# The value products of a step, moved behind the next step's first score

## What is computed

```python
q = (x @ q_w.T + q_b).reshape(B, S, H, Dh).transpose(0, 2, 1, 3)
k = (x @ k_w.T + k_b).reshape(B, S, H, Dh).transpose(0, 2, 1, 3)
v = (x @ v_w.T + v_b).reshape(B, S, H, Dh).transpose(0, 2, 1, 3)
q = apply_rope(q)
k = apply_rope(k)
attn = jnp.einsum('bhqd,bhkd->bhqk', q, k) * scaling
probs = jax.nn.softmax(attn, axis=-1)
out = jnp.einsum('bhqk,bhkd->bhqd', probs, v)
out = out.transpose(0, 2, 1, 3).reshape(B, S, D)
return out @ out_w.T + out_b
```

## Time and profile before

| | us |
|---|---|
| median of three runs | 868.22 |
| lowest, highest | 866.63, 878.57 |
| the profiled execution's own time | 867.31 |
| its span, first to last instruction | 865.6 |
| PE busy | 829.0 |
| DVE, ACT, POOL busy | 649.7, 525.2, 463.4 |
| mean granted clock of TensorE | 0.99 |

### The profile page before, as it was taken

How to read it: one execution, slowest core, us unless ns; L and a number is a source line. 1 busy time by engine, 2 the same in 40 slices (tenths; PEclk the granted TensorE clock), 3 DMA queues, 4 the chain that set the end, 5 groups by cost and what they waited for, 6 DMA issues and landing times.

```text
span 865.6 us, 14796 instructions
## 1 busy us (share of the span) xinstructions
PE 829.0 (96%) x4544; PEld 626.3 (72%) x4544; DVE 649.7 (75%) x1352; ACT 525.2 (61%) x1106; POOL 463.4 (54%) x397
## 2 busy tenths in 40 slices
PE   8899999999989999989998999999999989999997
PEld 6678788778878888766887888654434447888886
DVE  6898788999998888998386866757788644676553
ACT  4778788778868888763635442335566665454442
POOL 3565555666655556642666766522310526656774
PEclk9999999999999999999999999978999999999999
DMA  5233222322422323212765458311441133334451
GB/s 157 92 98 99 86 97 97 110 95 83 149 74 87 98 96 109 80 50 75 214 217 155 141 166 289 105 57 53 143 148 51 56 98 93 122 124 140 152 161 65
DMA packets 57442, 99.20 MB, mean 115 GB/s; under 512 B 8288, under 2 KB 19040, under 8 KB 57376
## 3 DMA queue, kind: packets, MB, share of 16 engines
q1 hardware_dynamic: 57376, 98.39, 35.5%
HBM read 71.88 MB, written 9.57 MB: 94 GB/s over the span
## 4 chain that ended last, share of the span: by engine, by line
PE 63%; POOL 10%; issue 10%; DVE 9%; ACT 4%; DMA 3%; SPq 0%; POOLq 0%; DVEq 0%; ACTq 0%
PE ps L986 10%; PE ps L972 9%; PE ps L963 9%; PE ps L321 5%; PE ps L387 5%; PE ps L335 4%; POOL q_sin L526 3%; PE ps L1654 3%; PE ps L375 3%; PE ps L348 3%; PE ps L1535 2%; PE ps L362 2%; POOL wqk_lo L520 2%; PE ps L1624 2%; DVE nm L1846 2%
## 5 line engine op out<-in xcount | busy, mean ns | idle before, releaser
L1110 POOL TENSOR_TENSOR ew_lo<-ew_raw,ew_hi 128x768 fp32r<-128x768 f32 x68 | 128.2, 1886 | 56.2 <-ACT ew_hi L1076 48.2
L1062 ACT ACTIVATE hid_hi<-guw 128x512 fp32r<-128x512 f32 x68 | 43.0, 632 | 156.6 <-POOL guw L1126 106.6
L1165 DVE TENSOR_TENSOR hid_lo<-guw,hid_hi 128x512 fp32r<-128x512 f32 x68 | 80.9, 1189 | 72.4 <-ACT hid_hi L1062 72.3
L1126 POOL TENSOR_TENSOR guw<-gu,cwb 128x512 f32<-128x512 f32 x61 | 80.5, 1320 | 91.3 <-issue 73.3
L526 POOL TENSOR_TENSOR q_sin<-q_sw,sin 128x512 f32<-128x512 f32 x62 | 80.7, 1312 | 52.5 <-DMA q_sw<-q_in 51.4
L1846 DVE TENSOR_REDUCE nm<-ps 128x1 f32<-128x512 f32 x128 | 81.6, 684 | 24.3 <-PE ps L1558 23.1
L1741 ACT ACTIVATE e<-ps 128x512 f32<-128x512 f32 x128 | 68.8, 602 | 40.3 <-PE ps L1654 40.1
L986 PE MATMUL ps<-ew_hi,hid_hi 128*128 128x256 f32 x272 | 78.3, 288 | 2.4 <-DVE hid_lo L1165 1.8
L512 DVE SCALAR_TENSOR_TENSOR w<-ex,rden,sgn 128x512 f32<-128x512 f32 (+3 forms) x128 | 79.0, 678 | 0.0
L438 ACT ACTIVATE ex<-sabs,nmax 128x512 f32<-128x512 f32 (+3 forms) x128 | 61.5, 551 | 27.9 <-DVE nmax L486 27.9
L986 PE MATMUL ps<-ew_hi,hid_lo 128*128 128x256 f32 x272 | 76.8, 282 | 0.0
(11 more groups left out here) (190 smaller groups left out, 2404.9 us busy)
## 6 DMA issues: line engine op xcount, KB each, us to landing
ew_raw<-in_ew SPq DMA_DIRECT2D x68, 384.0 KB, 3.3
q_sw<-q_in SPq DMA_DIRECT2D x128, 128.0 KB, 2.0
cwb<-cw_dram SPq DMA_DIRECT2D x61, 256.0 KB, 3.6
wqk_raw<-in_wqk SPq DMA_DIRECT2D x32, 256.0 KB, 2.7
wv_raw<-in_wv SPq DMA_DIRECT2D x32, 128.0 KB, 2.6
wo_raw<-in_wo SPq DMA_DIRECT2D x32, 128.0 KB, 2.2
qs<-stk_q SPq DMA_DIRECT2D x16, 256.0 KB, 3.6
ks<-stk_k SPq DMA_DIRECT2D x16, 256.0 KB, 4.2
```

What stands on the lines that cost most here:

```text
L1110: pool.tensor_tensor(ff[f].ew[1][:, i % EW_SLOTS, :], ew_raw[:, i % RAW_SLOTS, :], fp(ff[f].ew[0][:, i % EW_SLOTS, :]), ALU.subtract).then ...
L1126: pool.tensor_tensor(ff[f].guw[:, i % 2, :], ff[f].gu[:, i % 2, :], ff[f].cwb[:, r % CWB_SLOTS, :], ALU.mult).then_inc(sem("guw"), 1)
L1165: dve.tensor_tensor(ff[f].hid[1][:, i % 2, :], ff[f].guw[:, i % 2, :], fp(ff[f].hid[0][:, i % 2, :]), ALU.subtract).then_inc(sem("hid_lo"), 1)
```

## The change

The four value products of step s - 1 used to open step s. They now stand behind the first score of step s and behind slot 0. The read-out on ACT moves from behind the second exponential of its step to behind the third (`PV_AT + 2`). The numbers of instructions stay as they are; lines below 1324 of the changed kernel count one more.

```diff
@@ -1322,6 +1322,7 @@
         S_BANKS = 3
         S_BANK = (3, 0, 1)
         PV_BANK = 2
+        PV_AT = 0
         TAKEN_AT, ZT_AT, ZC_AT = 1, 1, 2
         ZT_TAIL, ZC_TAIL = 2, 3
@@ -1657,14 +1658,14 @@
             for n in range(S_BANKS):
                 scores(n)
             for s in range(STEPS):
-                if s > 0:
-                    for j in range(HEADS):
-                        pv_pe(pe, s - 1, j)
                 item = STEP_ITEM.get(s)
                 for j in range(HEADS):
                     if HEADS * s + j + S_BANKS < HEADS * STEPS:
                         scores(HEADS * s + j + S_BANKS)
                     slot_pe(pe, s, j)
+                    if s > 0 and j == PV_AT:
+                        for head in range(HEADS):
+                            pv_pe(pe, s - 1, head)
                     if (s, j) == (STEP_LOGIT, 2):
                         logits(pe, 1, 0)
                     if (s, j) == (STEP_LOGIT + 1, 0):
@@ -1739,7 +1740,7 @@
                     act.wait_ge(sem("st_ps"), n + 1)
                     wait(act, "pv1", HEADS * (s - 2) + j + 1)
                     act.activation(e1[:, s % 2 * HEADS + j, :], ps[:, S_BANK[n % S_BANKS], :], ACT.Exp, scale=SCALE1).then_inc(sem("e1"), 1)
-                    if j == 1 and s % QT == 0 and s > 0:
+                    if j == PV_AT + 2 and s % QT == 0 and s > 0:
                         read_out(act, s // QT - 1)
```

## The result

On one chip and in six executions each, the median is 873.72 us (872.79 to 878.47) against 869.55 us of the kernel before (864.09 to 878.57). So the change makes the kernel slower, by some 8 us or 0.9%. The sign was right and the time lies in the range, but the forecast cost, about 4 us, is half of what was measured. The profiled execution is the slowest of the six: 878.47 us, span 876.7, mean granted clock 0.981; that of before was 867.31 us, 865.6, 0.990. Four of its stretches at half clock, 3.4 us each, lie ahead of 400 us, where the change moves nothing. I therefore read places in it, and not its total.

A forecast was written before the change was run, and what follows sets the result against it. The prediction took TensorE (PE), busy 829.0 of 865.6 us, as the bound. Its nine terms sum to 4.05 us on the profiled 867.31, giving 871.4, taken as 871.5 us; forecast range 869 to 874.5, 8-in-10 range 866 to 875.5.

The forecast's parts named there:

- the ring: Light steps' cycle of value block, score, exponential, score, value block: still 2.62 us per step, so no change.
- 1, step 4, projection: After the layernorm's transposes PE waits for ACT at the first score, the block comes after, projection later: +0.85 us.
- 2, step 7, projection: Behind ACT's rounding copy that waits for POOL, the first score and block delay the projection a further +0.7 us.
- 3, step 8, read-out stall gone: Read-out step with a projection behind its third score: the held score now follows that projection, stall goes, -0.7 us.
- 4, step 9, transpose of the maxima: Block now queued behind the first maximum, which waits for the load of `ks`: transpose later by +1.1 us.
- 5, steps 10 to 13: A rounding copy's cost, a read-out stall gone and a projection held by DVE: 0 net.
- 6, step 19, output projection: ACT's chunk copy precedes exponential 76; the block no longer hides it, output projection later: +0.5 us.
- 7, DVE's chain, steps 21 to 25: DVE, busy without a gap up to the logits, gets its first maximum earlier; PE's losses there are covered: -0.2 us.
- 8, step 26, router's transposes: First score waits for exponential 104, behind that of the router's logits, and the block follows: transposes +0.8 us later.
- 9, step 29, gate: First score waits while ACT does the routing table and a weight copy; the block now follows it: +1.0 us.
- the read-out (0.61): Read-out steps, every fourth: the value bank's copy still delays a score as before, 0 change in light and read-out steps alone.
- the clock, priced as a rival: Longer waits behind the layernorm's transposes and near 680 us bring half clock, some 5 us lost, 876.5 us; chance 0.08.

The follow-up runs named there:

- f1: The changed kernel run once more, against the kernel before: 874.01 us, ratio 1.0081.
- g3: The kernel before with the value block moved in step 29 alone: 872.52 us, ratio 1.0033.
- e1: The kernel before with only the read-out moved behind the third exponential, value block left in front: 866.46 us, ratio 1.0004.
- f3: The kernel before with block and read-out moved only from step 25 on: 869.36 us, ratio 1.0026.
- e3: The change with the value block back in front in nine steps (4, 7, 9, 11, 12, 19, 25, 26, 29): 865.98 us, ratio 0.9982.
- g2: The change with the value block back in front in steps 9 and 29 alone: 869.87 us, ratio 0.9995.
- f2: The kernel before with block and read-out moved only in steps 1 to 13: 870.87 us, ratio 1.0049.
- g4: The kernel before with the value block moved in step 9 alone: 868.83 us, ratio 1.0036 [0.9999, 1.0073].
- e2: The change with the value block behind the first score but ahead of slot 0 and its first maximum, against the kernel before: 876.22 us, ratio 1.0128.
- g1: The change plus unread matmuls, ten before step 9's first maximum and seven before step 29's first score, against the kernel before: 872.27 us, ratio 1.0022.

## Why the prediction was half right

The terms in the order of the prediction. For terms 1 to 6 I set *f1* against *g3*, which has the old order up to step 28 and no half-clock stretch between 200 and 674 us. Each number is the further displacement at the next work outside the ring, after the 1.83 us by which the transposes of the layernorm already start later in *f1*. Terms 7 and 8 are read from the change against the kernel before, and term 9 from the router table's transposes (L932) to the gate, which is the same in the change, *f1* and *g3*.

| term | forecast | measured |
|---|---|---|
| 1, step 4, projection | +0.85 | +0.96 |
| 2, step 7, projection | +0.7 | +0.77 |
| 3, step 8, read-out stall gone | -0.7 | -0.90 |
| 4, step 9, transpose of the maxima | +1.1 | **+3.83**, 1.5 of it maximum, block and score at half clock |
| 5, steps 10 to 13 | 0 | +2.5, at half clock up to 625 us |
| 6, step 19, output projection | +0.5 | +0.1 |
| 7, DVE's chain, steps 21 to 25 | -0.2 | +0.4 to 0.6 (the change), -0.2 (*f1* against *g3*) |
| 8, step 26, router's transposes | +0.8 | +0.80 |
| 9, step 29, gate | +1.0 | +2.15, 1.1 of it half clock |

**Terms 1, 2, 3 and 8 held** to 0.2 us: a block of 1.0 us that had filled a wait for ACT is paid with its length, less what was idle before. So did the ring (2.61 us) and the read-out (0.61); the later read-out by itself (*e1*) brought no gain beyond the error. Term 6 was a little high: DVE held PE there as well. Term 7 depends on the pair that is compared: in the change PE gets to the last transpose of the maxima only at 686.91, 0.9 us after DVE is done with its input, since the block stands behind a first score that waited 1.23 us; in *f1* DVE is done later, and that covers it. Both are half a microsecond. Without its half-clock parts the column adds up to some 5.5 us, which is more than the 3.8 (good to 1.1) of *f1* at equal clock: single executions show one draw of each wait.

**The first failed step is term 4.** The prediction took the landing of `ks` as a fixed chain that shifts with the projection, from 619.15 to 619.9, and put the block's 1.0 on top. The landing isn't fixed: set against *g3*, it comes 3.83 us later in *f1*, where the projection of step 5, at the head of its chain, comes 2.80 later. SP reloads `ks` once the store of it has landed; its wait for that store, in the profile of before and then of the change:

```profile
SPq L1467 <- DMA stk_k<-qk_lo: 5.4, 1, 5.4
```

```profile
SPq L1468 <- DMA stk_k<-qk_lo: 6.9, 1, 6.9
```

Over the fourteen profiles this wait is 4.8 to 6.9 us; the kernel before happened to show one of the short ones. PE's idle time in step 9 with the block still in front was 0.55 us in the profile I read, but 0.93 and 1.43 in two other kernels that have the old order up to there (*g3*, *f3*), and 2.31, 2.03 and 1.30 in *e1*, *e3* and *g2*. With the block behind it was 3.28, 3.26 and 3.14 (the change, *f1*, *f2*), and 2.45 in *g4*. So the block's cover was worth its 1.0, as term 4 said, and about one more microsecond came from a wait that a single execution had shown at its smallest. The rest of the term is the clock.

**The second is the clock, priced as a rival at 0.08** and in the wrong place. The prediction looked for a fall behind the layernorm's transposes, of step 3 and "likewise near 680". Behind step 3, where the idle time went from 0.23 to 1.19 us, the clock stayed at 1.00. What the moved block brought were the falls of steps 9 and 29, and not as an accident of some executions: 0.0057 of the mean clock is missing over 12 of them, 3.9 us. The rival's size per fall (12 us at half clock, some 5 lost) was fair for step 9: 10.2 us of *f1* are at 0.50 from 615 on. What was missing was to ask it of every wait that the block had covered, those named in terms 4 and 9 first, and the loss belonged in the sum and not beside it. Had both stood there, 4 of order and 4 of clock, the sum would have been 875.3 from the profiled 867.3.

The Trainium skill's page "TensorE: Matmul & The Clock Gate" says in Part 1, of the ramp at a kernel's start, that it varies from run to run and that "the ramp penalty is <1% of a typical kernel span". It says this of the start; the 3.9 us lost here inside the kernel are 0.45% of the span as well, and half of what was to be predicted.

The profile of before had also shown an early half-clock stretch (575 to 589 us) which the change's has not. By the profiles alone it would seem that the stretch moved from there to step 9. In the other profiles with the old order up to step 9 it is absent there too (*e1*, *f3*, *g3*), and *e1* and *f3* show one at 616 to 619 and at 615 to 622 all the same. So the old order loses clock there as well, in some executions and for a shorter time. How often stays open, and with it the exact share of step 9 (*g4* didn't settle it) and of step 29.

**A third place falls whatever the order.** "Near 680" PE waits for DVE before the last transpose of the maxima. DVE's step ahead of it is a 16-column `nm_s` operation, 0.18 us elsewhere. It took 0.73 us in the profile of before and 4.26 in *g3*, though the order there is the same. DVE and POOL of before, then DVE, POOL and PE of *g3*:

```profile
678.33 0.73 DVE L1851 TENSOR_TENSOR nm_s<-nm 128x16 fp32r<-128x16 f32 x1
677.21 5.38 POOL L1110 TENSOR_TENSOR ew_lo<-ew_raw,ew_hi 128x768 fp32r<-128x768 f32 x3
671.68 4.26 DVE L1858 TENSOR_TENSOR nm_s<-nm 128x16 fp32r<-128x16 f32 x1
670.56 5.36 POOL L1110 TENSOR_TENSOR ew_lo<-ew_raw,ew_hi 128x768 fp32r<-128x768 f32 x3
676.21 0.40 PE L1568 MATMUL ps<-ident,nm_s 128*32 128x128 f32 x1 [2.35 <-DVE nm_s L1860]
```

In ten of the fourteen profiles the operation takes 4.1 to 4.3 us and ends within 0.05 us of the end of POOL's three weight operations; in the other four (before, the change, *e2*, *f3*) it takes 0.5 to 0.7 and the next one 1.7. That POOL holds it is argued from these times, since no run moves POOL's work. In eight of the ten no unread matmuls stand there (*e1*, *e3*, *f1*, *f2*, *g1* to *g4*): PE idles 1.0 to 2.5 us and falls to 0.50 between 675 and 693, with the block in front as well as behind. Of the four with the short operation none does, though the change falls at 693. So this loss of clock isn't the change's, but it moves single profiles against one another.

## What to carry to other kernels

Before work is moved behind a wait, list each place where that work had been filling a wait, and price it there: its own length, plus the clock that such waits have cost elsewhere, in this trace or another of the same kernel. Read a wait for a DMA as a spread and not as a number: one profiled execution shows one draw of it. Stalls that are removed from a ring of two engines needn't bring a gain (*e1*); and putting other work between two matmuls that run side by side can cost a slot (*e2*).

## What the runs showed of the hardware

- Single waits of 3.26 and 3.28 us (step 9), 2.45 (*g4*) and 1.89 us (step 29), in stretches where PE was otherwise busy, were followed by 7 to 10 us at 0.50. Waits of 1.19 and 1.01 us in steps 4 and 7 were not. With unread matmuls in the waits of steps 9 and 29 the clock stayed at 1.00 at both (*g1*, whose profile has its longest fall, 13.7 us, near 680). The length of the wait alone doesn't decide it: in step 9, waits of 2.31 us (*e1*), 2.03 (*e3*), 1.43 (*f3*), 1.30 (*g2*) and 0.90 (*e2*) had 3.4 to 6.8 us at 0.50 behind them, and 0.93 (*g3*) and 0.55 (before) none.
- An execution of this kernel costs 6.8 us for each 0.01 of mean granted clock: 0.01 of some 866 us is 17.3 us at half clock, in which a PE that never idled would lose 8.7, so by this estimate four fifths of a fall are paid. PE is busy 95% of the span.
- A score and a maximum side by side start together and take 0.33 us for the pair (611.22 to 611.55 in the profile of the change); put apart by the value block in one of four pairs they cost the light step 0.23 us (*e2*).
- A DVE operation of 16 columns took 0.18 us in most places, and 4.1 to 4.3 us where it began beside POOL's three weight operations of 128 x 768 and ended with them (ten profiles); the cause is argued, not tested.
